# A two-stage attention and expert kernel on one core: the layer-norm statistics of x are taken one batch ahead, those of the attention output and the seeds move to other steps

## The reference, cut to what matters

```
x = x + layernorm(attention(layernorm(x)))      # 16 heads of 16, softmax over 1024 keys, biases
x = x + layernorm(experts(layernorm(x)))        # 16 experts, top 8 by a normalised gate, one shared expert
layernorm(x) = (x - mean) / sqrt(var + 1e-5)
```

## Time and profile before

| | us |
|---|---|
| median of 3 runs | 2789.33 |
| the profiled execution, whole | 2794.4 |
| its span, first to last instruction | 2792.5 |
| PE busy in it | 2700.3 |
| DVE busy | 2203.7 |
| ACT busy | 1628.2 |
| POOL busy | 1040.4 |

### The profile page before, as it was taken

How to read it: one execution, slowest core, us unless ns; L and a number is a source line. 1 busy time by engine, 2 the same in 40 slices (tenths; PEclk the granted TensorE clock), 3 DMA queues, 4 the chain that set the end, 5 groups by cost and what they waited for, 6 DMA issues and landing times.

```text
span 2792.5 us, 49038 instructions
## 1 busy us (share of the span) xinstructions
PE 2700.3 (97%) x17634; PEld 1775.7 (64%) x17634; DVE 2203.7 (79%) x4585; ACT 1628.2 (58%) x3159; POOL 1040.4 (37%) x1057
## 2 busy tenths in 40 slices
PE   5999999999999999999998999999999999999997
PEld 3445445454454444544543488888888888888886
DVE  5799999989989999999899566666666666666654
ACT  1588888878878788788788733333333333333332
POOL 4042563644635636545358353111111111111112
PEclk8899999999999999999999999999999999999999
DMA  5102333122122222330232323222222222223222
GB/s 119 27 28 58 70 76 72 57 62 66 43 66 66 69 65 64 73 66 28 66 93 76 94 71 101 80 71 75 84 84 82 75 76 84 80 69 84 80 73 54
DMA packets 126595, 197.39 MB, mean 71 GB/s; under 512 B 12288, under 2 KB 74768, under 8 KB 124304
## 3 DMA queue, kind: packets, MB, share of 16 engines
q1 hardware_dynamic: 126352, 194.25, 26.8%
HBM read 108.74 MB, written 17.30 MB: 45 GB/s over the span
## 4 chain that ended last, share of the span: by engine, by line
PE 80%; DVE 13%; ACT 3%; issue 2%; POOL 1%; DMA 0%; POOLq 0%; SPq 0%; ACTq 0%; DVEq 0%
PE o_bank L597 14%; PE y_bank L775 14%; PE g_bank L761 13%; PE u_bank L761 13%; PE st_bank L568 10%; DVE score_max L1164 10%; PE sm_bank L587 8%; PE job_bank L587 2%; ACT probs L1056 2%; PE sm_bank L693 2%; PE job_bank L693 1%; DVE qk_parts L1187 1%; PE job_bank L716 1%; PE job_bank L729 0%; DVE row_max L1171 0%
## 5 line engine op out<-in xcount | busy, mean ns | idle before, releaser
L1056 ACT ACTIVATE probs<-st_bank 128x512 f32<-128x512 f32 x2023 | 1079.2, 603 | 268.9 <-PE st_bank L568 258.6
L1164 DVE TENSOR_REDUCE score_max<-sm_bank 128x1 f32<-128x512 f32 x1601 | 1023.3, 681 | 69.5 <-PE sm_bank L587 63.6
L568 PE MATMUL st_bank<-qk_stack 64*128 64x512 f32 x2023 | 743.4, 427 | 7.1 <-ACT probs L1056 6.9
L587 PE MATMUL sm_bank<-qk_stack 64*128 64x512 f32 x1601 | 655.8, 461 | 27.8 <-DVE score_max L1164 22.1
L597 PE MATMUL o_bank<-probs,v_quad 128*32 128x512 f32 x4096 | 552.7, 612 | 0.7 <-ACT probs L1056 0.7
L568 PEld LDWEIGHTS st_bank<-qk_stack 64*128 64x128 f32 x2023 | 350.2, 186 | 274.7 <-ACT probs L1056 232.6
L587 PEld LDWEIGHTS sm_bank<-qk_stack 64*128 64x128 f32 x1601 | 288.7, 189 | 296.8 <-DVE score_max L1164 268.3
L1312 DVE TENSOR_TENSOR h<-gate_act,u_bank 128x512 f32<-128x512 f32 x256 | 176.2, 688 | 310.9 <-ACT gate_act L1010 310.7
L1010 ACT ACTIVATE gate_act<-g_bank 128x512 f32<-128x512 f32 x272 | 162.4, 597 | 416.0 <-PE u_bank L761 415.9
L1021 ACT ACTIVATE h_hi<-h 128x512 fp32r<-128x512 f32 x272 | 172.1, 633 | 327.8 <-DVE h L1315 290.2
L1595 POOL TENSOR_SCALAR f_x_in<-f_x_in,f_mv,f_rstd 128x256 f32<-128x256 f32 x64 | 90.3, 1422 | 617.2 <-DVE f_rstd L1226 617.2
(11 more groups left out here) (248 smaller groups left out, 4854.6 us busy)
## 6 DMA issues: line engine op xcount, KB each, us to landing
cb<-comb_dram SPq DMA_DIRECT2D x256, 256.0 KB, 3.5
qk_stack<-qk_parts SPq DMA_DIRECT2D x180, 256.0 KB, 5.5
x_in<-in_x SPq DMA_DIRECT2D x8, 1024.0 KB, 5.5
o_part<-o_sb SPq DMA_DIRECT2D x64, 128.0 KB, 2.7
sum_part<-o_sb SPq DMA_DIRECT2D x64, 128.0 KB, 2.8
x_res<-in_x SPq DMA_DIRECT2D x16, 512.0 KB, 3.9
x<-x_res SPq DMA_DIRECT2D x16, 512.0 KB, 4.1
f_x_in<-x SPq DMA_DIRECT2D x16, 512.0 KB, 3.9
```

Of the source, the lines that this page charges most:

```text
L568: mm(bank_of(tile)[:, :], k_stack[q][p][rows, kc * CH:(kc + 1) * CH], q_stack[q][p][rows, f * HALF:(f + 1) * HALF], start=True, stop=True) ...
L587: mm(shared_bank[bank][:, :], q_stack[q][p][rows, tok:tok + CH], k_stack[q][p][rows, half * HALF:(half + 1) * HALF], start=True, stop=True ...
L1056: nc.scalar.activation(probs[kc % 2][:, HEAD_AT[j], :], bank_of(4 * U + j)[:, :], ACT.Exp).then_inc(exp_done, 1)
L1164: v.reduce_max(score_max[f][:, HC * (2 * p + e) + c, half:half + 1], shared_bank[max_bank[n]][:, :], AX_X).then_inc(smax_read, 1)
```

## The change

X statistics of batch b + 2 are now taken in batch b, at u43, 44, 45, 47, 48, 50, 51 and 52, with the seed at u55. Only batch 0 keeps the old units too, for batch 1. The eight statistics of the attention output move by up to five units, and the seed "a1" from u40 to u46. On GpSimd the residual of the second half of batch b - 1 moves behind the next `split_lo(b, 1, 0)`; on SyncE its store moves behind `gather(b, 5)` and `load_shift(b, 7)`. In the last batch VectorE's part of the gate weights (`gT_lo`) comes one unit sooner. No count of instructions changes.

```diff
--- before.py
+++ after.py
@@ -57,13 +57,16 @@
         for _part in range(2):
             JOBS[_u + _part] = (_kind, _off, _i + _n, _part)
 
-X_STATS = {0: 0, 2: 1, 5: 2, 6: 3, 7: 4, 8: 5, 9: 6, 10: 7}
-A_STATS = {14: (0, 0), 15: (0, 1), 17: (0, 2), 20: (0, 3), 30: (1, 0), 32: (1, 1), 36: (1, 2), 38: (1, 3)}
+
+X_STATS = {43: 0, 44: 1, 45: 2, 47: 3, 48: 4, 50: 5, 51: 6, 52: 7}
+FIRST_X_STATS = {0: 0, 2: 1, 5: 2, 6: 3, 7: 4, 8: 5, 9: 6, 10: 7}
+FIRST_X_SEED = 16
+A_STATS = {15: (0, 0), 16: (0, 1), 19: (0, 2), 20: (0, 3), 33: (1, 0), 36: (1, 1), 41: (1, 2), 42: (1, 3)}
 
 SPLITS = {39: (0, 0, 0), 46: (0, 1, 0), 3: (-1, 0, 1), 11: (-1, 1, 1)}
 
 RECIPS = {27: (0, 0, 0), 35: (0, 1, 0), 59: (0, 0, 1), 4: (-1, 1, 1)}
-SEEDS = {16: "x", 21: "a0", 40: "a1"}
+SEEDS = {55: "x", 21: "a0", 46: "a1"}
 
 FIRST_JOBS = [("XT", i) for i in range(4)] + [("QK", i) for i in range(8)]
 PER_BATCH = {"XT": 4, "QK": 8, "V": 4, "SH": 8, "OP": 4}
@@ -479,10 +482,10 @@
                 if not last:
                     load_stack(b + 1, 0, False)
                     load_stack(b + 1, 1, False)
+                gather(b, 5)
+                load_shift(b, 7)
                 if not first:
                     store_x1(b - 1, 1)
-                gather(b, 5)
-                load_shift(b, 7)
                 if last:
                     for e in range(EARLY, ALL_E):
                         load_w(e)
@@ -1365,8 +1368,8 @@
                         gate_step(2 * (u - 15) + n)
                 if u == 22:
                     gate_step(12)
-                if u in (47, 49):
-                    gT_lo((u - 47) // 2)
+                if u in (46, 48):
+                    gT_lo((u - 46) // 2)
                 if u in (50, 51):
                     for n in range(6):
                         norm_step(0, 6 * (u - 50) + n)
@@ -1429,20 +1432,24 @@
                     if u in RECIPS and not (first and RECIPS[u][0]):
                         off, f, k = RECIPS[u]
                         sum_recip(b + off, f, k)
-                    if not last and u in X_STATS:
-                        ln_x_stats(b + 1, X_STATS[u])
+                    for B, table in ((1, FIRST_X_STATS if first else {}), (b + 2, X_STATS)):
+                        if B < BATCHES and u in table:
+                            ln_x_stats(B, table[u])
                     if not first and u in A_STATS:
                         ln_a_stats(b - 1, *A_STATS[u])
+                    if first and u == FIRST_X_SEED:
+                        seed_x(1)
                     if u in SEEDS:
                         if SEEDS[u] == "x":
-                            if not last:
-                                seed_x(b + 1)
+                            if b + 2 < BATCHES:
+                                seed_x(b + 2)
                         elif not first:
                             seed_a(b - 1, int(SEEDS[u][1]))
                     if maxima:
                         reduce(S + 2, (s + 2) % STEPS, kc, 1, among_scores(u, first, last))
-                    if not last and u in X_STATS:
-                        ln_x_aggr(b + 1, X_STATS[u])
+                    for B, table in ((1, FIRST_X_STATS if first else {}), (b + 2, X_STATS)):
+                        if B < BATCHES and u in table:
+                            ln_x_aggr(B, table[u])
                     if not first and u in A_STATS:
                         ln_a_aggr(b - 1, *A_STATS[u])
                     if last:
@@ -1639,12 +1646,12 @@
                         weight_lo(e)
                 divide(b, 1, 0)
                 split_lo(b, 0, 0)
-                if not first:
-                    residual(b - 1, 1)
                 if last:
                     for e in range(6, EARLY):
                         weight_lo(e)
                 split_lo(b, 1, 0)
+                if not first:
+                    residual(b - 1, 1)
                 if not last:
                     for q in range(3):
                         copy_v(b + 1, q, False)
```

## The result

Changed 2771.04 us (median of 5 runs, 2769.39 to 2775.10), before 2794.86 on the same chip (5 runs, 2788.68 to 2798.21): ratio 0.9921, interval 0.9903 to 0.9938. That is 0.8% faster, and outside my range of 2774 to 2798. The profiled execution took 2769.65 us (span 2767.9, mean clock 0.989), before 2794.4 (2792.5, 0.984).

What follows compares the result with a forecast made beforehand. PE, with 80% of the chain, was taken to bound the kernel, in turns with VectorE in the attention. Terms -17.4 + 11.1 + 0.6 + 0.9 - 1.0 - 1.2 = -7.0 from 2794.4 gave 2787.4, stated as 2787, range 2774 to 2798 us.

Steps and rivals of the forecast that it cites:

- Part 1: u38 to u42, batches 1 to 6: without the seed and the long u40 it makes, 14.75 us per batch, -17.4 us.
- Part 2: Seed "a1" at u46, batches 1 to 6: GpSimd holds it, third reduction 2.4 us late, 1.85 per batch, +11.1 us.
- the signs that I had named against it: Wrong if u46 stays under 3.5, the seed there takes 0.5, or u43 to u45 exceed 3.1.
- Part 7: Last batch: u40 from 4.00 to near 2.75, seed at u46 +1.3, gT_lo sooner at most 1 us; in sum 0.
- Parts 3 to 6: X statistics in V units +0.6, seed at u55 +0.9, u0 to u3 -1.0, u30 to u33 -1.2, queues 0.
- The rival "swallowed": At u46, idle times near 0.5 us in every V unit and PE's four banks absorb the collision: 2776 us; chance 0.21.
- The half clock moves along: PE idles at u46 to u47 as at u40, 1.5 us in most batches, 2.8 in one: 2795 us; chance 0.13.
- the V units break: X statistics make PE wait for banks in each V unit, 48 x 0.41 = 19.7 us: 2807 us; chance 0.10.
- GpSimd's phase shifts: row_max at u7, u31, u39, u63: a 0.3 us shift makes or saves up to 1 us each; no separate chance.

Runs made afterwards that it cites:

- the probe: Not the reference kernel: eight large GpSimd instructions beside VectorE's row of 72 small ones; 59 small ones beside four tensor_scalar, 10 beside four tensor_tensor.
- e4: Changed kernel with gT_lo back at u47 and u49: 2776.27 us, ratio 0.9943 to the kernel before, 5.2 us more than the changed kernel.
- e8: Kernel before with only the last batch's gT_lo one unit sooner: 2787.4 us, ratio 0.9978 to the kernel before.
- e6: Changed kernel with four more bn_stats on VectorE ahead of the seed at u46 in batches 0 to 5: 2788.6 us, 17.6 more than the changed kernel.
- e2: Kernel before with only the x statistics and seed of x moved a batch ahead, "a1" still at u40: 2790.18 us, ratio 0.9999.
- e1: Kernel before with only the seed "a1" at u46, its residual and store moved along: 2777.62 us, ratio 0.9949.
- e3: Changed kernel with seed "a1" back at u40 and its statistics at u30, 32, 36, 38: 2790.63 us, 19.6 more than the changed kernel.
- e9: Changed kernel with reciprocals one unit sooner at u26, u34, u58, the last batch's u27 and u35 kept: 2763.55 us, ratio 0.9890.

## Why the prediction was wrong

- Part 1, the hole at u40: right (-16.9 for -17.4). The 0.5 us missing stand in u42, which I had put near 0: it takes 3.06 us with a statistic against 2.95, 0.1 in each batch. One reading was loose: PE had not "stood idle for much of u40", but for 0.74 of 4.86 us.
- Part 2, the seed at u46: **this step failed**, +11.1 us forecast for +0.1. Two of the signs that I had named against it came: u46 under 3.5 (2.94), and a seed of 0.5 us. The text had it that "the first instruction ends at 605.96", with GpSimd's first. I had carried the rule from u40, where an instruction that started 1.18 us into a GpSimd tensor_scalar was held to its end, to one that starts at 0.56. u46 and the probe show two held stretches and a free one between; the seed's first two instructions fell in the free one. That spared the meeting with L1565's tensor_tensor, which I had made the larger half of the 2.4 us, and the reduction ran beside the third. The conversion of delay to time was sound: 1.07 of 1.60 and 2.28 of 2.8 us in two experiments, delay less 0.5. I had taken 1.85 of 2.4.
- Part 7, "gT_lo sooner: no work, at most 1 us either way": **the second failure**, by 6.3 us in the profiled execution (5.2 and 6 in the medians of e4 and e8), over half as large. I priced the wait it removes and not the clock behind it, although the same trace had shown PE losing the clock behind u40 and I had counted 7.4 us for that. I had not read the granted clock of the attention's last 37 us. By e6, part of this size is a matter of the execution.
- Parts 3 to 6: right within 0.7 us in sum, the queues at nothing included. e2 shows that the largest part of the diff, the x statistics, moves the time by about 0.1% at most.
- The rival "swallowed" (2776) named what happened at u46: idle times near 0.5 us in every V unit took the delay up, but of a delay five times smaller. With -6.3 for the gate it would have said 2770, against 2769.65 profiled. So the miss of part 2 alone would have ended inside my range, and the gate took the time out of it. "The half clock moves along" and "the V units break" did not come about; e6 shows the first does once the seed is late enough. "GpSimd's phase shifts" did not either: u7, u31 and u63 are the same within 0.02 us in batch 2. The 5.1 us by which the profiled execution of before lay above the median of three runs came down to between -0.5 and 3.4 with more runs of it.
- Still open: why the half clock in the kernels with the hole falls on other batches from one kernel to the next (most often at u41, but at u32 of batch 6 in e1, e2 and e3, e1 without the hole), and why e6 and e9 had one at the end of the attention with no wait for gT_lo.

## What to carry to other kernels

A small instruction held by another engine is priced by where it starts inside the other's instruction, so the starts must be worked out in the new place, and a hold seen at one phase isn't carried to another. When a change removes a wait of PE, read the granted clock of the stretch behind it before saying that it is worth its own length, and read it in several kernels, since one execution can lose the clock where the next does not. A late engine costs its delay less the idle time standing in the unit (here 0.5 us), so a first question is whether the delay is below that.

## What the runs showed of the hardware

A GpSimd tensor_scalar of 1.56 us holds VectorE's small tensor_scalar from 0.11 to 0.71 us and again from 0.95, and leaves it free between; in the second hold further small instructions start but end with the first, while a reduction from PSUM ran beside the held one (u46). Beside it VectorE's tensor_tensor was held once, for 0.59 us, at its start. A GpSimd tensor_tensor of 1.27 us holds both kinds for the whole instruction. With a wait of 1.37 us on PE in front of one small matmul, the work up to the first expert matmul took 4.9 us longer at a mean grant of 0.83 than without it at 1.00; in one run (e6) the grant was 0.83 there without that wait. At u40, where the longest wait of PE was 0.61 us, the clock cost between nothing and 2.8 us more, by batch.
